# Second attention of a two-layer gated block: the output bias added by a fourth product on TensorE instead of an addition to x on GpSimd

## The reference, cut to what matters

```python
x = x + tanh(g_xattn[0]) * L0_attention(...)
x = x + tanh(g_ffn[0])   * L0_experts(layernorm(x))
x = x + tanh(g_xattn[1]) * L1_attention(layernorm(x), ctx, ctx)
x = x + tanh(g_ffn[1])   * L1_experts(layernorm(x))

# L1_attention
q, k, v = query @ Wq + bq, key @ Wk + bk, value @ Wv + bv
attn = softmax((q . k + q . rel_k[ids]) / sqrt(8))
out = attn . v + attn . rel_v[ids]
return out.reshape(B, Sq, H) @ Wo + bo
```

## Time and profile before

| | us |
|---|---|
| median of 3 runs (lowest, highest) | 2222.26 (2221.87, 2222.7) |
| profiled execution: its time | 2223.91 |
| profiled execution: span of its instructions | 2222.1 |
| PE busy, DVE busy, ACT busy, POOL busy | 2087.2, 1916.7, 1554.5, 1597.9 |

### The profile page before, as it was taken

The page is one execution under the profiler, slowest core; times in us unless marked ns, Lnnn a source line. Parts: engine busy times, 40 slices in busy tenths (PEclk is TensorE's granted clock), DMA queues, the critical chain, the costliest instruction groups (busy, mean ns, idle before and its releaser), DMA issues. The chain is left out here.

```text
span 2222.1 us, 82115 instructions
## 1 busy us (share of the span) xinstructions
PE 2087.2 (94%) x28058; PEld 1635.8 (74%) x28060; DVE 1916.7 (86%) x4322; ACT 1554.5 (70%) x3452; POOL 1597.9 (72%) x1521
## 2 busy tenths in 40 slices
PE   3999999977999999999995999999999976999999
PEld 1788888854666666666663999999999973666666
DVE  5899999987888888898895888888888878888888
ACT  3788888865556565555553777777777756888887
POOL 1577777643666666666665999999999943888887
PEclk9899999987999999999997999999999988999999
DMA  5000000004332332222321455555555530000000
GB/s 155 11 6 6 6 6 6 7 1 97 90 89 76 85 85 79 86 83 77 90 66 36 77 78 78 78 78 78 78 78 78 80 74 8 10 14 14 9 14 14
DMA packets 476442, 121.39 MB, mean 55 GB/s; under 512 B 431879, under 2 KB 446855, under 8 KB 475604
## 3 DMA queue, kind: packets, MB, share of 16 engines
q1 hardware_dynamic: 343988, 86.86, 18.5%
q10 hardware_dynamic: 132384, 33.63, 6.6%
HBM read 106.51 MB, written 13.89 MB: 54 GB/s over the span
## 5 line engine op out<-in xcount | busy, mean ns | idle before, releaser
L1219 POOL TENSOR_TENSOR f_low<-f_hidden,f_high 128x512 f16<-128x512 f32 x336 | 442.3, 1321 | 217.3 <-ACT f_high L1151 215.4
L1177 DVE TENSOR_TENSOR f_hidden<-f_hidden,f_share 128x512 f32<-128x512 f32 x336 | 374.1, 1114 | 0.0
L1366 POOL TENSOR_TENSOR f_low<-f_hidden,f_high 128x512 f16<-128x512 f32 x256 | 296.4, 1159 | 74.4 <-ACT f_high L1309 74.2
L1157 ACT ACTIVATE f_act_out<-f_gate 128x512 f32<-128x512 f32 x336 | 200.4, 596 | 192.6 <-PE f_gate L1121 192.6
L1200 DVE SCALAR_TENSOR_TENSOR f_hidden<-f_up,f_act_out 128x512 f32<-128x512 f32 x336 | 229.8, 684 | 82.7 <-PE f_up L1121 50.6
L1742 POOL TENSOR_TENSOR a_q_head_high<-a_q_t_high,a_head_mask 128x2048 f16<-128x2048 f16 x64 | 233.0, 3640 | 55.3 <-PE a_score L1544 47.2
L1151 ACT ACTIVATE f_high<-f_hidden 128x512 f16<-128x512 f32 x336 | 210.5, 627 | 72.9 <-DVE f_hidden L1177 71.6
L1131 PE MATMUL f_y<-w_high,f_high 128*128 128x128 f16 x1344 | 242.4, 219 | 2.2 <-POOL f_low L1219 2.2
L1131 PE MATMUL f_y<-w_low,f_high 128*128 128x128 f16 x1344 | 242.4, 219 | 0.0
L1131 PE MATMUL f_y<-w_high,f_low 128*128 128x128 f16 x1344 | 242.4, 219 | 0.0
L1742 POOL TENSOR_TENSOR a_q_head_low<-a_q_t_low,a_head_mask 128x2048 f16<-128x2048 f16 x64 | 232.8, 3637 | 0.0
(11 more groups left out here) (269 smaller groups left out, 8521.2 us busy)
## 6 DMA issues: line engine op xcount, KB each, us to landing
f_share<-expert_shares SPq DMA_DIRECT2D x128, 256.0 KB, 3.2
a_q_pos<-queries ACTq DMA_DIRECT2D x64, 512.0 KB, 3.9
f_share<-expert_shares SPq DMA_DIRECT2D x128, 128.0 KB, 3.1
relative_values<-a_rel_all SPq DMA_DIRECT2D x512, 8.0 KB, 1.7
x_all<-in_x SPq DMA_DIRECT2D x4, 1024.0 KB, 8.1
f_share<-expert_shares SPq DMA_DIRECT2D x128, 32.0 KB, 1.8
queries<-a_q_parts SPq DMA_DIRECT2D x64, 64.0 KB, 4.0
a_rel<-relative_values SPq DMA_DIRECT2D x64, 64.0 KB, 3.2
```

The source lines that it names most:

```text
L1157: nc.scalar.activation(act_out[m % RING][:, :], gate_ps[m % BANKS][:, :], ACT.Silu, scale=1.0 / WSCALE).then_inc(act_ready, 1)
L1177: nc.vector.tensor_tensor(hidden[r][:, :], hidden[r][:, :], share[k][:, :, :].rearrange("p t q -> p (t q)"), ALU.mult).then_inc(scaled, 1)
L1219: nc.gpsimd.tensor_tensor(low[r][:, :], hidden[r][:, :], high[r][:, :], ALU.subtract).then_inc(low_ready, 1)
L1366: nc.gpsimd.tensor_tensor(low[k][:, :], hidden[k][:, :], high[k][:, :], ALU.subtract).then_inc(low_ready, 1)
```

## The change

The output projection of the second attention gets a fourth product: `sel` times a new tile `out_rows`, which holds the constant row in two fp16 parts as `bias_rows` does. `add_bias` and its semaphore go. In the block's beginning VectorE makes `out_rows` from `b_o` in four steps that wait for one another, behind L1799 and ahead of the slots. TensorE waits once for them, in the projection of batch 0 (slot 4).

```diff
@@ fin_project (TensorE)
+                        if isinstance(n, int) and n == 0:
+                            pe.wait_ge(out_bias, 4)
                         for k, (m, w) in enumerate(products(mixed_t[p], w_out)):
-                            mm = nc.tensor.matmul(fin_ps[:, 0:D], m[:, :], w[:, :], start=(k == 0), stop=(k == 2))
+                            nc.tensor.matmul(fin_ps[:, 0:D], m[:, :], w[:, :], start=(k == 0), stop=False)
+                        mm = nc.tensor.matmul(fin_ps[:, 0:D], sel[:, :], out_rows[:, :], start=False, stop=True)
                         mm.then_inc(y_ready, 1)
@@ GpSimd
-                def add_bias(n):
-                    if inside(n, 0, B):
-                        pool.wait_ge(xn_ready, n + 1)
-                        nc.gpsimd.tensor_tensor(x_all[:, n, :], x_all[:, n, :], b_o[:, :], ALU.add).then_inc(x_biased, 1)
                 def slot(n, p):
                     mask_queries(n + 1, o)
                     add_relative(n - 3, o)
-                    add_bias(n)
                     divide(n - 3, o)
@@ VectorE, behind L1799
+                dve.wait_ge(weights_ready, 3)
+                nc.vector.tensor_copy(out_rows[:, :], b_o[:, :]).then_inc(out_bias, 1)
+                dve.wait_ge(out_bias, 1)
+                nc.vector.tensor_tensor(b_o[:, :], b_o[:, :], out_rows[:, :], ALU.subtract).then_inc(out_bias, 1)
+                dve.wait_ge(out_bias, 2)
+                nc.vector.tensor_scalar(b_o[:, :], b_o[:, :], ident[:, 1:2], None, ALU.mult).then_inc(out_bias, 1)
+                dve.wait_ge(out_bias, 3)
+                nc.vector.scalar_tensor_tensor(out=out_rows[:, :], in0=out_rows[:, :], scalar=ident[:, 0:1], in1=b_o[:, :],
+                                               op0=ALU.mult, op1=ALU.add).then_inc(out_bias, 1)
@@ residual (VectorE)
                         dve.wait_ge(y_ready, n + 1)
-                        dve.wait_ge(x_biased, n + 1)
```

More of the change, by code:

```diff
@@ L1426, in relative_attention @@
         sel, bias_rows = sb("sel", [P, P], F16), sb("bias_rows", [P, D], F16)
+        out_rows = sb("out_rows", [P, D], F16)
         prob = [sb(f"prob{k}", [P, 4, KC]) for k in range(4)]
@@ L1454, in relative_attention @@
         mixed_turned, mixed_high, mixed_low = sem("mixed_turned"), sem("mixed_high"), sem("mixed_low")
-        y_ready, x_biased, x_ready = sem("y_ready"), sem("x_biased"), sem("x_ready")
+        y_ready, x_ready, out_bias = sem("y_ready"), sem("x_ready"), sem("out_bias")
         SCALE = float(HD) ** -0.5
```

## The result

| | before | changed |
|---|---|---|
| median of 11 runs each (lowest, highest) | 2222.7 (2221.42, 2226.53) | 2228.53 (2227.27, 2231.99) |
| ratio, 95% interval | | 1.0025 (1.0016 to 1.0034) |
| profiled execution: its time | 2223.91 | 2227.27 |
| profiled execution: span | 2222.1 | 2225.5 |

The changed kernel is slower, by 5.8 us in the medians. The forecast was 2226.0, and the median came out 0.3 us above the top of its range. The interval of the ratio is +3.6 to +7.6 us, so it just holds the 3.74 us of the sum. The two profiled executions are only 3.4 us apart. A profile is a single execution, though: that of the changed kernel is the fastest of its eleven, and that of the kernel before lies 1.2 us above its median. Single executions of one kernel scatter here with a standard deviation of 1.1 to 2.4 us, so two profiles alone can't decide about 2 us.

The account below looks back on a forecast made before the run. The prediction took TensorE's stream of columns to bound the second attention's slots. Its terms, 3.3 + 0 + 0.33 + 0.11 = 3.74 us, took the median from 2222.26 to 2226.0 us, with a range of 2223.6 to 2228.2.

Parts of the forecast that it names:

- the sum: Whole kernel: the terms 3.3, 0, 0.33 and 0.11 us add up to 3.74 us more.
- What bounds the kernel: Second attention's slots: TensorE is the bound, by the columns it streams; GpSimd has about 0.8 us to spare a slot.
- Part 1: Packed slots: the added fourth product costs TensorE 0.055 us in each of 60 slots, +3.3 us.
- Part 2: GpSimd's slots: removing the 0.458 us addition only adds idle time there, worth 0.
- Part 3: Block's beginning: the four VectorE steps, mostly hidden by idle time, delay the first scores, +0.33 us.
- Part 4: Draining: the added product disappears in slots 64 to 66 and costs one step in slot 67, +0.11 us.
- The edge: `relative` 1 products behind ScalarE's copy: TensorE loses 0.08 us every second slot (0.47 and 0.55 us); pattern expected unchanged.
- Rival A: At `relative` 1, ScalarE's copy comes late in every slot: 2.4 us more, total +6.1, 2228.4 us; chance 0.06.
- Rival C: Filling: later first scores delay the clock's rise, up to 1.6 us more, total +4.1 to +5.3; chance 0.09.
- the one from the sum to the time: Whole kernel: 3.74 us added to the median of 3 runs, 2222.26, gives 2226.0 us, or +0.17%.

Follow-up runs that it names:

- no_addition: Kernel before without GpSimd's addition of the output bias and the waits for it, bias left out of the result; 2225.62 us, ratio 1.0000.
- product_x8: Kernel before, addition kept on GpSimd, plus eight products of `sel` and zeros in each output projection; 2252.21 us, ratio 1.0123.
- rows_moved: Kernel before without the query projection's bias product from slot 0 on; VectorE adds that bias, ScalarE rounds, GpSimd forms the low part; 2219.11 us, ratio 0.9975.
- after: The changed kernel in its first measurement, against the kernel before; 2228.53 us, ratio 1.0025.
- again_after: The changed kernel run again, unaltered, against the kernel before in another set; 2230.63 us, ratio 1.0030.
- third_after: The changed kernel run a third time, unaltered, against the kernel before; 2228.35 us, ratio 1.0019.
- after_once: Changed kernel with the router-score stage's 4 KB constant loaded once and kept in SBUF; 2228.23 us, ratio 1.0020 to the kernel before.
- after_pad: Changed kernel with twenty unread products in TensorE's idle time ahead of the second attention; 2228.57 us, ratio 1.0016 to the kernel before.
- second_after_once: Changed kernel with the 4 KB constant loaded once, run again beside the changed kernel on one chip; 2228.3 us, ratio 1.0022 to the kernel before.
- before_once: Kernel before with the router-score stage's 4 KB constant loaded once and kept in SBUF; 2224.45 us, ratio 1.0006.
- after_pad64: Changed kernel with 64 unread products in TensorE's wait after its block has begun; 2226.98 us, ratio 1.0014 to the kernel before.
- before: The kernel without the change, in the first measurement; 2222.7 us.
- again_before: The kernel before run again, unchanged, as a control against itself; 2224.97 us, ratio 1.0001.
- pad_before: Kernel before with ten unread products in TensorE's idle time ahead of the second attention; 2225.39 us, ratio 1.0008.
- product_added: Kernel before, addition kept on GpSimd, plus one product of `sel` and zeros in each output projection, without the four VectorE steps; 2228.55 us, ratio 1.0017.

## Why the prediction was wrong, by its own steps

**What bounds the kernel:** right that it is TensorE, which is busy for 460.00 of 460 us in both kernels. The addition on GpSimd was worth nothing (`no_addition`, 1.0000), and a product more or less on TensorE moved the time by its own step, up (`product_x8`) and down (`rows_moved`). Too wide is the prediction's "the bound of the slots is the number of columns". The steps follow the columns for the fp16 products of 64 columns and more (medians from 1300 to 1760: 0.029 us for 64, 0.035 for 77, 0.056 for 128), but the 32 mixing products of a slot, with 9 and 18 columns, take 0.062 us each, more than the added product. Here are three of these and two scores, before:

```profile
1503.99 0.20 PE L1580 MATMUL a_mix<-a_value,a_prob_t_low 77*128 77x9 f16 x1
1504.05 0.21 PE L1578 MATMUL a_mix<-a_value,a_prob_t_high 77*128 77x18 f16 x1
1504.11 0.20 PE L1580 MATMUL a_mix<-a_value,a_prob_t_low 77*128 77x9 f16 x1
...
1504.35 0.20 PE L1542 MATMUL a_score<-a_k_t_low,a_q_head_high 128*128 128x77 f16 x1
1504.39 0.20 PE L1542 MATMUL a_score<-a_k_t_high,a_q_head_low 128*128 128x77 f16 x1
```

The forecast was right all the same, since it priced the product by neighbours of its own form.

**Part 1, 3.3 us:** right. The step is 0.055 us; the packed slots grew by 2.8 to 3.3 us over 56 slots, and the period of two slots by 0.09 to 0.13 us (medians 18.47 and 18.49 us before, 18.60 and 18.58 with the change).

**Part 2, 0:** right, as far as the slots and the times show.

**Part 3, 0.33 us:** right as a term: the first scores start 12.18 us behind `a_fin<-a_w_o` instead of 11.86 us. As the cost of the filling it was too small, since it had no room for what varies there. In the six executions whose four steps stand at the beginning and whose clock wasn't raised by padding (`after`, `again_after`, `third_after`, both of `after_once`'s kind, `after_pad`) the filling took 50.46 to 51.41 us, mean 50.83; in the seven that lack the steps (`rows_moved` not counted) it took 50.14 to 50.37, mean 50.18. That is +0.65 us, twice the term. In two of the six, `third_after` and `after_pad`, TensorE waits within the filling for the reload of a batch's queries (`a_q_pos`), and their fillings, 51.41 and 51.32 us, are the longest. Here is `third_after`, waits from 1222 to 1260:

```profile
PE a_score L1543 <- DMA a_q_pos<-queries: 0.6, 1, 0.6
```

In `second_after_once` and in `before_once`, which has no steps, the first scores are released by such a reload, and come 0.1 to 0.2 us later than in the others. Whether the 0.33 us brought the waits on, or whether they come by chance, the runs don't say.

**Part 4, 0.11 us:** right: the draining went from 6.58 to 6.69 us in each of the profiles of the two kernels.

**The edge, Rival A:** 0.48 and 0.55 us, unchanged; A did not happen. **Rival C:** its mechanism was seen, its price wasn't. The mean clock from 1220 to 1230 fell from 0.84 to 0.70, a rise from 1.2 to 2.4 GHz that comes 2.8 us later and holds back some 1.4 us of the stream; but the wait of 1.28 us for the exponential shrank to 0.2 us with it, and the two nearly cancel. Neither rise belongs to one kernel alone: `after_once`, with the four steps, had it early (0.86, the wait of 1.3 us, and 50.46 us of filling, against 50.56 in `after`), and `no_addition`, without them, had it late (50.37 us against 50.14). But the late rise, 17.2 to 18.2 us behind the block's start instead of 14.4 to 14.9, came in five of the six executions with the steps and in one of the seven without, so the change may well favour it. Its price was 0.0 to 0.2 us where no other wait came with it. With 64 unread products ahead of the block the clock from 1205 to 1220 was 0.73 instead of 0.50, and the filling 49.81 us. That is 0.7 of the 1.3 to 1.4 us by which `after_pad64` is better than its neighbours; the rest no row shows.

**The sum, 3.74 us:** the block's profiles agree with it, within a scatter of about 1 us. From its start to the router the changed program took 623.75 to 627.92 us in five executions (`after`, `again_after`, `third_after`, `after_once`, `second_after_once`), mean 625.2, and the program of before (or one with the same products in TensorE's slots) 620.11 to 622.57 in five (`before`, `again_before`, `no_addition`, `pad_before`, `before_once`), mean 621.4: +3.8. The 627.92 us are those of `second_after_once`, in which the clock fell at the loop's entry, as its windows show:

```profile
1264.40:1271.20 6.80, 6.80 (x87) 6.61 (x84) 3.68 (x9) 2.91 (x9) 6.61 (x2) 0.50 0.37 41
```

6.8 us at 0.50 hold back 3.4 us of the stream. Without this execution the mean is 624.6 and the difference 3.2 us.

**The step that failed** is the one from the sum to the time, "the median of 3 runs, 2222.26, goes to 2226.0", and the range made from it. First, it had no term for the scatter of a median. Three runs gave 2222.26, and 11 to 30 runs of the same kernel 2222.7, 2223.53, 2223.88, 2224.41 and 2224.6; the forecast's base was lower than all of them. Against the 2222.7 beside which the changed kernel was measured the sum gives 2226.4. Second, Part 3 as the cost of the filling was 0.33 us and measured 0.65. Third, it treated everything outside the four parts as fixed to 0.1 us. In the profiles the block starts anywhere from 1206.3 to 1210.8 us, the entry of the loop takes 18.5 to 19.9 us (22.6 once), and the load behind the router is late by 1.8 us or isn't. Of the 2.5 us between 2226.0 and 2228.53 the base is 0.4 and the filling 0.3; the other 1.8 us have no place. The bounds were uneven as well: the 2224.9 has about 0.5 us for the runs' own spread below 3.0 and 0.11 us, the 2227.2 has almost none above 3.6, 1.17 and 0.11; with the same it would be 2227.6. That Rival A's 2228.4 lies next to the measured time is chance, since its mechanism did not happen.

**What stays open:** the changed kernel against the kernel before gave +5.8, +6.0 and +4.5 us in three sets; by means +5.7, +6.3 and +4.1, and, with the scatter of each weighed, +5.3 with an interval of 4.7 to 5.9. The sets, of which the second and the third ran on different chips, differ by more than that scatter explains (2.2 us between the second and the third, with a standard error of 0.7), so the true interval is wider, and the third alone agrees with the sum. The sum is short of the mean by about 1.5 us. `product_added` and `after_once` had +3.95 and +4.7, without the four steps or without the load, and `after_once` against `before_once` +3.8; none of these is measured finely enough to say that it gave the 1.5 us back. The profiled executions don't hold it: in the two pairs their spans differ by 3.4 and 2.9 us, but there the changed kernel was caught at its fastest and the kernel before above its median. It may be the filling's extra waits, the late load (a third more of the executions would be 0.5 us, an estimate from 13 profiles), the loop's entry, or the chip, each in some share. That was argued and not shown.

## What to carry to other kernels

When one engine's stream is packed, price an edit by start-to-start steps of that stream. That was exact here to 0.01 us a product, for one and for eight of them, and it pointed to the better kernel: move constant additions off the bound engine, not onto it. Take the step from a product of the same form: one of 9 columns cost more here than one of 128. For an effect of 4 us in 2200, first measure how far the base itself moves between sets of runs and chips, and put that into the range. Before a profile is used to explain a median, see where its own time lies among the runs. And before instructions of VectorE are moved off a path, look at what GpSimd does at the new place: 0.3 us each became 3.6.

## What the runs showed of the hardware that was not expected

- Three short VectorE instructions beside GpSimd's multiplications of 3.63 us took 2.25, 3.62 and 3.53 us instead of 0.23 to 0.29, among them a subtraction with both inputs in SBUF; each ended 0.08 to 0.15 us behind the GpSimd instruction it lay beside.
- In TensorE's packed stream a fp16 product of 9 or 18 columns took 0.062 us from start to start, one of 64 columns 0.029, one of 77 columns 0.035, one of 128 columns 0.056.
- A load of 4 KB was used 1.6 to 2.3 us behind its issue, or 3.3 to 3.5 us when a 16 KB fetch of instructions started about 1 us behind the issue (five of five between 0.98 and 1.44 us).
- The clock's rise in the filling came about 3 us later in `after` than in `after_once` and cost 0.1 us, since a wait for ScalarE shrank from 1.3 us to 0.2 us. A fall to 0.50 for 6.8 us in the loop's entry, which one execution of 16 had, cost some 3.4 us.
- The medians of one kernel differed by up to 1.9 us (2222.7 to 2224.6) between sets of 11 to 30 runs, each later set on another chip.
